# Bias in a freed row of the contraction, and expert weights loaded per block from DRAM

## The reference

```python
xn = layernorm(x)                              # 16 x 256 tokens, D = 128: each row sums to 0
s = attn(xn)                                   # mLSTM attention, 4 heads, normalised per head
logits = xn @ router_w + router_b
top1 = argmax(softmax(logits))                 # 8 experts, one for each token
h = xn @ w1[top1] + b1[top1]                   # 128 -> 1024
a, g = split(h, 2)
y = (a * sigmoid(g)) @ w2[top1] + b2[top1]     # 512 -> 128
out = x + s * silu(y)
```

## Time and profile before

| | us |
|---|---|
| median of 3 runs (281.29 to 282.22) | 281.92 |
| span of the profiled execution | 281.2 |
| PE busy | 246.7 |
| DVE busy | 191.9 |
| ACT busy | 166.7 |
| POOL busy | 125.1 |

### The profile page before, as it was taken

How to read it: one execution, slowest core, us unless ns; L and a number is a source line. 1 busy time by engine, 2 the same in 40 slices (tenths; PEclk the granted TensorE clock), 3 DMA queues, 4 the chain that set the end, 5 groups by cost and what they waited for, 6 DMA issues and landing times.

```text
span 281.2 us, 6001 instructions
## 1 busy us (share of the span) xinstructions
PE 246.7 (88%) x1640; PEld 210.6 (75%) x1640; DVE 191.9 (68%) x637; ACT 166.7 (59%) x511; POOL 125.1 (44%) x163
## 2 busy tenths in 40 slices
PE   0499969999999999999999999699999999997860
PEld 0379956776677677678889999699999899996510
DVE  3995264367764454455578798969999988967092
ACT  0143063775578778778577777377676677782030
POOL 5352000233588887884102432624463436537241
PEclk9996565697999999999999999799999999999995
DMA  7799995423144354455000110110112011000395
GB/s 201 213 368 336 288 180 83 146 77 118 53 164 136 122 147 145 122 145 153 14 1 21 50 43 28 39 56 15 52 40 60 19 53 48 21 25 16 112 313 173
DMA packets 31008, 30.92 MB, mean 110 GB/s; under 512 B 3294, under 2 KB 25830, under 8 KB 30976
## 3 DMA queue, kind: packets, MB, share of 16 engines
q1 hardware_dynamic: 27456, 26.19, 33.6%
q0 software_dynamic: 2272, 4.22, 4.3%
q10 hardware_dynamic: 1248, 0.13, 0.3%
HBM read 21.58 MB, written 9.41 MB: 110 GB/s over the span
## 4 chain that ended last, share of the span: by engine, by line
PE 59%; DVE 18%; issue 7%; DMA 4%; ACT 4%; SPq 2%; DVEq 2%; POOL 1%; ACTq 0%; POOLq 0%
PE bank L1033 15%; PE bank L1042 10%; PE bank L1001 10%; PE bank L959 8%; PE bank L900 3%; DVE dm L838 3%; DMA x_sb<-in_L_attn_x 2%; PE bank L938 2%; PE bank L942 2%; PE bank L987 2%; ACT dm L530 2%; DVE xw L595 2%; PE bank L1007 2%; DMA xw<-y_tokens 2%; PE bank L894 1%
## 5 line engine op out<-in xcount | busy, mean ns | idle before, releaser
L1033 PE MATMUL bank<-qm,wc 128*128 128x128 f32 x624 | 77.0, 276 | 0.6 <-DVE wc L711 0.6
L402 POOL DMA_INDIRECT y_tokens<-qm,xs_sb x39 | 41.7, 1070 | 75.5 <-DVE qm L855 72.9
L1033 PEld LDWEIGHTS bank<-qm,wc 128*128 128x128 f32 x624 | 73.4, 193 | 1.0 <-DVE wc L711 1.0
L1042 PE MATMUL bank<-w_sb,dm 128*128 x312 | 43.3, 283 | 5.6 <-DVE dm L838 5.2
L838 DVE SCALAR_TENSOR_TENSOR dm<-bank,wc,dm 128x128 f32<-128x128 f32 x156 | 43.7, 343 | 4.9 <-ACT dm L530 4.8
L530 ACT ACTIVATE dm<-bank,wc 128x128 f32<-128x128 f32 x156 | 43.9, 364 | 1.1 <-PE bank L1033 1.1
L1042 PEld LDWEIGHTS bank<-w_sb,dm 128*128 128x128 f32 x312 | 38.7, 195 | 7.7 <-issue 7.6
L462 ACT ACTIVATE qm<-bank 32x256 f32<-32x256 f32 x64 | 24.0, 375 | 21.4 <-PE bank L938 20.8
L397 POOL DMA_INDIRECT xs_sorted<-xw,pos x32 | 31.4, 982 | 11.5 <-issue 8.1
L478 ACT ACTIVATE dm<-mb,tm 128x128 f32<-128x128 f32 x120 | 36.5, 390 | 0.0
L959 PE MATMUL bank<-qm,xnT 128*128 128x512 f32 x64 | 32.9, 637 | 0.0
(11 more groups left out here) (168 smaller groups left out, 343.2 us busy)
## 6 DMA issues: line engine op xcount, KB each, us to landing
mb<-minus_max SPq DMA_DIRECT2D x15, 512.0 KB, 3.9
w_sb<-in_L_ffn_w SPq DMA_DIRECT2D x8, 512.0 KB, 7.5
xs_sorted<-pad_row SPq DMA_DIRECT2D x1, 2515.5 KB, 19.7
xs_sb<-xs_sorted SPq DMA_DIRECT2D x13, 193.5 KB, 2.5
x_sb<-in_L_attn_x SPq DMA_DIRECT2D x8, 256.0 KB, 4.9
xw<-y_tokens SPq DMA_DIRECT2D x8, 256.0 KB, 4.4
out_x<-xw SPq DMA_DIRECT2D x8, 256.0 KB, 3.4
y_tokens<-qm,xs_sb POOLq DMA_INDIRECT x39, 2.3
```

What stands on the lines that cost most here:

```text
L402: pool.indirect_dma_start(y_dram, bass.IndirectOffsetOnAxis(ap=xs_sb[:, j // CH % NX, j % CH, D:DW].bitcast(I32), axis=0), ys_sb[:, j // C ...
L1033: last = pe.matmul(bank[2 * (j % 2) + k][:, c * P:(c + 1) * P], wc[:, j % 3, m:m + P], xsT[:, j % 2, :], start=True, stop=True)
L1042: last = pe.matmul(bank[6 + j % 2][:, 0:D], uT[:, j % 2, c, :], w2_sb[:, bass.ds(e * (HC * D) + c * D, D)], start=(c == 0), stop=(c == HC ...
```

## The change

Each row of `xn` sums to 0, so its last element is minus the sum of the others. With row 127 of `w1[e]` subtracted from rows 0 to 126, the last element isn't needed, and row 127 of the contraction is free: `xsT` gets 1.0 there, and the folded weights get `b1[e]`. So the biases of `product` and of the sigmoid go, and each becomes one instruction over 512 columns. The folded weights of all experts are written to DRAM, and for each block SP reads the expert's number into a register and loads 512 KB from there into `wc`.

DVE makes the subtraction (`fold_row`) behind the outputs of batches 4 to 11, one expert each. SP loads row 127, broadcast to all partitions, into the three `wc` buffers in turn, and writes the eight folded matrices behind the last load of `mb`. The loads of token rows and of weights share SP's list: first four chunks of rows, then the weights of each block, and behind those of blocks 7, 10, and so on up to 31 a further chunk of rows.

```diff
@@ sync engine @@
             for e in range(E):
-                sp.dma_start(w1_sb[:, e, 0:H2], w1[e]).then_inc(s_w1, 16)
+                sp.dma_start(w1_sb[:, e, :], w1[e]).then_inc(s_w1, 16)
...
                 sp.dma_start(mb[:, b % 2, :, :], m_dram[NH * b:NH * (b + 1), :].partition_broadcast(P)).then_inc(s_mb[b % 2], 16)
-
-            sp.wait_ge(s_scat, 16 * T)
-            for c in range(NCH):
+                if b == 1:
+                    sp.wait_ge(s_w1, 16 * E)
+                    sp.dma_start(w1_sb[P - 1:P, :, :], b1.unsqueeze(0)).then_inc(s_b1, 16)
+                e = b - 1 if b <= 3 else b - 4
+                if e < 3 and b <= 3 or 3 <= e < E:
+                    if e >= 3:
+                        sp.wait_ge(s_sub, e - 2)
+                    sp.dma_start(last_row[:, e % 3, :], w1[e, D - 1:D, :].partition_broadcast(P)).then_inc(s_bc[e % 3], 16)
+
+            sp.wait_ge(s_b1, 16)
+            for e in range(E):
+                sp.wait_ge(s_sub, e + 1)
+                sp.dma_start(w1_dram[e], w1_sb[:, e, :]).then_inc(s_wd, 16)
+
+            def load_rows(c):
                 if c >= NX:
                     sp.wait_ge(s_xsp, (c - NX + 1) * CH)
                     sp.wait_ge(s_yst[c % NX], 16 * CH * (c // NX))
...
+            def load_w(j):
+                e = sp.value_load(bexp_i[0:1, j:j + 1], min_val=0, max_val=E - 1)
+                if j >= 3:
+                    sp.wait_ge(s_h, j - 2)
+                sp.dma_start(wc[:, j % 3, :].unsqueeze(1), w1_dram[bass.ds(e, 1), :, :].rearrange("e p h -> p e h")).then_inc(s_wl[j % 3], 16)
+
+            sp.wait_ge(s_scat, 16 * T)
+            for c in range(NX):
+                load_rows(c)
+            sp.wait_ge(s_bexp, 1)
+            sp.wait_ge(s_wd, 16 * E)
+            for j in range(NBLK):
+                load_w(j)
+                if j % CH == 1 and NX <= (j + 5) // CH < NCH:
+                    load_rows((j + 5) // CH)
@@ pool: one more memset @@
+            pool.memset(xsT[:, :, :], 1.0).then_inc(s_ones, 1)
@@ scalar engine: copy_w and the b1 load are gone @@
-                act.activation(xsT[:, j % 2, :], bank[4][:, 0:P], ACT.Copy).then_inc(s_xse, 1)
+                act.activation(xsT[0:P - 1, j % 2, :], bank[4][0:P - 1, 0:P], ACT.Copy).then_inc(s_xse, 1)
...
-                    for c in range(HC):
-                        last = act.activation(sg[:, j % 2, c, :], bank[2 * (j % 2) + 1][:, c * P:(c + 1) * P], ACT.Sigmoid,
-                                              bias=wc[:, j % 3, H2 + HC + c:H2 + HC + c + 1])
-                    last.then_inc(s_th, 1)
+                    act.activation(sg[:, j % 2, :, :].rearrange("p c t -> p (c t)"), bank[2 * (j % 2) + 1][:, :],
+                                   ACT.Sigmoid).then_inc(s_th, 1)
@@ vector engine: copy_w and L612 are gone @@
+                    elif b - 4 < E:
+                        fold_row(b - 4)
+
+            def fold_row(e):
+                if e == 0:
+                    dve.wait_ge(s_w1, 16 * E)
+                dve.wait_ge(s_bc[e % 3], 16 * (e // 3 + 1))
+                w = w1_sb[0:P - 1, e, :]
+                dve.tensor_tensor(w, w, last_row[0:P - 1, e % 3, :], ALU.subtract).then_inc(s_sub, 1)
...
-                for c in range(HC):
-                    last = dve.scalar_tensor_tensor(uT[:, j % 2, c, :], bank[2 * (j % 2)][:, c * P:(c + 1) * P],
-                                                    wc[:, j % 3, H2 + c:H2 + c + 1], sg[:, j % 2, c, :], ALU.add, ALU.mult)
-                last.then_inc(s_uu, 1)
+                flat = "p c t -> p (c t)"
+                dve.tensor_tensor(uT[:, j % 2, :, :].rearrange(flat), bank[2 * (j % 2)][:, :], sg[:, j % 2, :, :].rearrange(flat),
+                                  ALU.mult).then_inc(s_uu, 1)
@@ tensor engine: the b1 transpose is gone @@
-                pe.wait_ge(s_wc, j + 1)
+                pe.wait_ge(s_wl[j % 3], 16 * (j // 3 + 1))
...
-                    if k == 0:
-                        pe.wait_ge(s_wv, j + 1)
```

More of the change, by code:

```diff
@@ L59, in mlstm_moe_block @@
     y_dram = nc.dram_tensor("y_tokens", (NTOK, D), F32).ap()
+    w1_dram = nc.dram_tensor("w1_folded", (E, P, H2), F32).ap()
     m_dram = nc.dram_tensor("minus_max", (R, S), F32).ap()
@@ L79, in mlstm_moe_block @@
         u_all = sb("u_all", [P, T, NH, DA])
-        w1_sb = sb("w1_sb", [P, E, WB])
-        wc = sb("wc", [P, 3, WB])
+        w1_sb = sb("w1_sb", [P, E, H2])
+        wc = sb("wc", [P, 3, H2])
+        xsT = sb("xsT", [P, 2, D])
         w2_sb = sb("w2_sb", [P, E * HC * D])
@@ L174, in mlstm_moe_block @@
         sy = qflat[:, 8 * D:10 * D].rearrange("p (i d) -> p i d", i=2)
-        xsT = qflat[:, 10 * D:12 * D].rearrange("p (i d) -> p i d", i=2)
         sg = dm[:, 0, :, :, :]
         uT = dm[:, 1, :, :, :]
+        last_row = wc
         wflat = dm[:, 1, :, :, :].rearrange("p k h s -> p (k h s)")
@@ L200, in mlstm_moe_block @@
         s_w2 = sem("s_w2")
+        s_b1 = sem("s_b1")
+        s_bc = [sem(f"s_bc{i}") for i in range(3)]
+        s_sub = sem("s_sub")
+        s_wd = sem("s_wd")
+        s_wl = [sem(f"s_wl{i}") for i in range(3)]
         s_chain = sem("s_chain")
@@ L268, in mlstm_moe_block @@
         s_out = sem("s_out")
-        NSMALL = 11
+        NSMALL = 10
         block = ctx.enter_context(nc.Block())
@@ L495, in attention @@
                         decay(b + 1)
-            act.wait_ge(s_ones, 2)
+            act.wait_ge(s_ones, 3)
             attention()
[L499 to L509, removed]
             def evac_xs(j):
@@ L610, in _ @@
                               wbd[:, :].rearrange("p (h d) -> p h d", h=NH),
[L611 to L612 removed]
+                              vmean[:, :].unsqueeze(2).to_broadcast([P, NH, DH]), ALU.add).then_inc(s_wts, 1)
             dve.wait_ge(s_lg, 1)
@@ L670, in _ @@
             dve.wait_ge(s_tm, 1)
-            dve.wait_ge(s_ones, 2)
+            dve.wait_ge(s_ones, 3)
             def routing(part):
@@ L857, in _ @@
             dve.wait_ge(s_w2, 32)
+            dve.wait_ge(s_bexp, 1)
             normals = normalise_all(range(len(GROUPS)))
@@ L917, in _ @@
             pe.transpose(bank[4][:, P:2 * P], natbd[:, 2, :], ident[:, :])
-            pe.transpose(bank[4][:, 2 * P:2 * P + 2 * NH], gates_raw[:, 0:D], ident[0:2 * NH, 0:2 * NH])
-            pe.transpose(bank[5][:, 0:E * (WB - H2)], b1_nat[:, :], ident[0:E * (WB - H2), 0:E * (WB - H2)]).then_inc(s_wT, 1)
+            pe.transpose(bank[4][:, 2 * P:2 * P + 2 * NH], gates_raw[:, 0:D], ident[0:2 * NH, 0:2 * NH]).then_inc(s_wT, 1)
             keep_warm(2, 7)
@@ L1017, in _ @@
             pe.matmul(bank[7][:, E * T:2 * E * T], tril[:, :], ohf, start=True, stop=True).then_inc(s_cnt, 1)
-            pe.wait_ge(s_ones, 2)
+            pe.wait_ge(s_ones, 3)
             attention()
```

22 lines of the change are left out of this document (removed).

## The result

| | before | changed |
|---|---|---|
| median, us (range) | 281.56 (278.85 to 282.22) | 297.7 (295.97 to 299.02) |
| span of the profiled execution | 281.24 | 294.2 |

With the runs made beside the changed kernel, before has five. The changed kernel takes 1.0625 times as long (1.0564 to 1.0687). The forecast was 286.9 with a range up to 295: the sign is right, the size is not. The device time lies 1.75 us above the span in each execution. That puts the profiled one of before at about 283.0, above all five of its times, while that of the changed kernel is the lowest of its five; so the traces differ by 13.0 us and the medians by 16.1. What follows explains the 13.0. Ratios compare fast executions alone: one that took over 1.5% more than the fastest of its kernel is left out.

A forecast was written before the change was run, and what follows sets the result against it. Prediction: POOL bounds the attention's even batches, PE the experts' stage, with 11.0 us of stalls mostly behind DVE. -10.5 - 1.0 + 8.0 + 5.0 + 1.5 + 2.0 = +5.0 us gives 286.9 us, range 279 to 295.

The forecast's parts named there:

- folds: Attention: each of eight DVE subtractions holds POOL's L379 up by 1.0 us, and POOL has no slack; +8.0 us.
- start of the experts' stage: First L1033 waits for the eight writes, then a register read and block 0's weight load; +5.0 us (2.5 to 9).
- slow clock there: Start of the experts' stage: PE runs slow behind a gap without work; +1.5 us (0 to 3).
- gaps behind row chunks: Experts' loop: at every third block a weight load queues behind SP's y scatter wait; 4.5 x 0.4 = +2.0 us.
- DVE's relief: Experts' stage: DVE saves some 1.1 us a block, giving back 10.5 of 11.0 us of stalls; -10.5 us.
- behind the last L1042: End of the kernel: the silu and the four last scatters come earlier; -1.0 us (0 to -2).
- the third rival: Experts' loop: loads bound it, sharing DMA engines; stall 2.1 instead of 0.4, 9.5 us in all, 294.4; chance 0.15.
- L379 starts where `fold_row` ends: Attention, expected sign in the changed profile: POOL's L379 begins at the fold's end, about 1.0 us late.
- folds cost nothing: Attention, rival: POOL is already in its next batch before a fold, or isn't blocked; 278.9 us; chance 0.17.
- The clock didn't fall behind the folds: Attention, rival denied here: pauses at folds put PE's clock down at half of the eight; +5.6, 292.5; chance 0.10.
- The relief was no smaller than it looked: Experts' stage, rival denied here: DVE stays late for normalising steps, 5 of 11 us come back; 292.4; chance 0.05.

The follow-up runs named there:

- e1_rows_later: Changed kernel with SP issuing each later chunk of token rows three blocks later, same bytes; 285.47 us, ratio 1.0177 to the kernel before.
- e6_fixed_expert: Changed kernel with the expert of SP's weight load fixed as j modulo 8, no register read, wrong weights for most blocks; 294.13 us, ratio 1.0351.
- e10_quarter_loads: Changed kernel with each block's weight load cut to a quarter of the columns, 128 KB instead of 512, SP's list unchanged; 287.42 us, ratio 1.0162.
- e2_no_fold: Changed kernel with the fold's subtraction replaced by a copy of one element per partition, waits, writes and loads kept; 289.1 us, ratio 1.0279.
- e3_fold_after_evac: Changed kernel with fold_row moved ahead of the outputs, where POOL is in its scatters; 297.33 us, ratio 1.0633.
- e4_early_writes: Changed kernel with each folded matrix written one batch behind its fold and the first three weight loads ahead of the token rows; 287.67 us, ratio 1.0256.
- e5_both: Changed kernel with later row chunks three blocks later, early writes, and the first three weight loads ahead of the token rows; 279.28 us, ratio 0.9898.
- the better kernel: Changed kernel with folds moved ahead of the attention and weights copied on chip by DVE and ScalarE, no folded weights in DRAM; 273.29 us, ratio 0.9679.

## Why the prediction missed the size

The terms of the sum, on the profiled executions, which differ by 13.0 (12.9 by the rounded terms):

| term | forecast | measured |
|---|---|---|
| folds | +8.0 | +5.7 |
| attention begins earlier | 0 | -0.4 |
| start of the experts' stage | +5.0 | +6.5 |
| slow clock there | +1.5 | +2.1 |
| gaps behind row chunks | +2.0 | +9.3 |
| DVE's relief | -10.5 | -10.7 |
| behind the last L1042 | -1.0 | +0.35 |
| sum | +5.0 | +12.9 |

*Gaps, the step that failed in size.* The mechanism was written out: the load of block j+1 behind a wait for a scatter of block j-5, at every third block. Its series was too short at each link. For block 14, t0 is 183.18, the end of block 10's hidden. The scatter of block 8 was issued at 185.48, t0 + 2.3 (forecast 2.4). It landed at 188.75, t0 + 5.6 (5.0): 3.3 us, where I had taken 2.6 from a view of before in which little ran beside it (2.1 to 3.2, with a DMA share of 0.11). Rows were issued at 188.81, the load at 189.95, t0 + 6.8 (5.8): a register read of 0.7 us where I had put 0.4 for read and issue. It landed at 194.21, t0 + 11.0 (9.8), in 4.26 us instead of 3.9 and a little. PE wanted it at 189.93 + 2.79 = 192.72, t0 + 9.5 (9.4). The stall was so small a difference of two large sums (0.4) that 1.2 us more in the first made it 1.6; that it is gone at every other place held roughly (five gaps of 1.56 on the mean, four of 0.2). I had this case as the third rival, with a load at t0 + 11.5, 9.5 us and a chance of 0.15. That should have been the forecast: the scatter's landing and the load's had been priced on rows with less traffic, the register read by guess, and the change itself brings the traffic. To say "the traffic is under the rate above" answered whether the bytes fit, not how long one transfer then takes. e1_rows_later takes out the wait, e6_fixed_expert the register read and e10_quarter_loads most of the bytes; each shrinks the gaps, the first and the last to nothing or nearly so.

*Folds.* The mechanism was right (e2_no_fold), and so was reading the scatter's row at 163.56 for it (e3_fold_after_evac). The size was 0.7 a batch instead of 1.0: I had L411 start as the fold ends, but it starts 0.36 us into the fold and ends 0.26 us behind it, so what counts is its stretching from 0.42 to 1.12 us. "L379 starts where `fold_row` ends" was wrong in this detail.

*Start.* The writes ran at 354 GB/s, faster than the 325 taken, but the first landed only 5.5 us after its issue instead of about 3.6 by my figures; on the old clock the last was there at 140.6 (139.4 forecast). That first write was issued 0.43 us behind the last `mb` load, which itself took 4.6 us to land. The register read and the issue took 1.04 instead of 0.4, the landing 3.4 instead of 3.9. That the token rows queue behind the writes I had said, but not that PE would stand for them first: 3.32 us, ahead of the 2.58 for the weights. e4_early_writes shows that all this and the slow clock vanish if the writes are begun behind their folds and the first loads go ahead of the rows.

*Slow clock.* It is at 0.50 from 144.7 to 154.9; the first two periods cost 1.8 and 0.3. It fell in the 3.32 us without work ahead of the token rows, and was down already when the 2.58 us ahead of the first hidden began. The length of a pause alone doesn't tell what follows: waits of 1.42 to 1.66 us in the loop left the clock at 1.00, those of 2.03 (e4_early_writes) and 2.08 us (e6_fixed_expert) stood right ahead of a stretch at 0.50, and the 0.70 us of the earlier trace rows, from which I had worked, ended 1.8 us ahead of one.

*Relief.* 10.7 against 10.5: the stage takes 119.5 us from the first to the last group, 107.8 at the pace of 2.79, plus 9.3 of gaps, 2.1 of clock and 0.3 of DVE. That a DVE with slack would leave no stalls was right, to 0.3 us. But I had read the stalls of before as a DVE with too much to do, and named POOL's gamma product for the row at 254.20 alone. The stall at 180.26 also stands behind a DVE step, one of the normalisation, that is held up beside a gamma product, in before:

```profile
176.06 3.03 DVE L562 TENSOR_SCALAR ra<-veps 128x32 int32<-128x32 int32 x1
...
176.66 2.38 POOL L410 TENSOR_TENSOR u_all<-cm,gamma 128x1024 f32<-128x1024 f32 x1
```

Such a step takes 0.18 us elsewhere. The stalls behind the four gamma products of before (at 176.66, 206.15, 233.16 and 253.72, with DVE instructions of 3.03, 2.13, 1.73 and 2.06 us beside them) add up to 7.2 of its 11.0 us. In e5_both the same four meetings are there, and PE keeps its pace:

```profile
180.65 2.37 POOL L445 TENSOR_TENSOR u_all<-cm,gamma 128x1024 f32<-128x1024 f32 x1
...
180.85 2.22 DVE L579 TENSOR_SCALAR ry<-ra 128x32 int32<-128x32 int32 x1
...
180.99 1.95 PE L1041 MATMUL bank<-xsT,wc 128*128 128x128 f32 x16
183.78 1.95 PE L1041 MATMUL bank<-xsT,wc 128*128 128x128 f32 x16
```

So what the lighter DVE buys is mostly the slack that takes four blocks of 2 us. Whether the kernel before would gain as much with its gamma products placed elsewhere was not tried.

*End.* I had the last silu and scatters come earlier behind the last L1047. They don't: the first of the four comes behind POOL's gamma product at 266.77 and the DVE product L863 that it held up for 1.78 us, and from there they are a series of POOL's own with 0.3 between them. Before, the same series held only 0.4 us more of waiting.

*The other rivals.* That folds cost nothing fell with e2_no_fold. The clock didn't fall behind the folds: it is 1.00 over the eight batches with PE waiting about 0.6 us for L411 in each. The relief was no smaller than it looked.

*Range.* The terms' errors don't cancel: the gaps are 7.3 over, start, clock and end 3.5, the folds 2.3, the attention's earlier beginning 0.4 and the relief 0.2 under, 7.9 in all. The rest of the 10.8 us by which the median missed is where the profiled executions lie among their runs. I had set the span of before beside the median, as if it were that execution's time, and called it 0.7 under; with the 1.75 us around it, it is 1.4 over. What makes runs of one kernel differ by this much isn't known from these traces. The range ended at 295 because only one of the open terms was taken at its upper end at a time.

## What to carry to other kernels

A load in an in-order issue list inherits every wait ahead of it. Give a wait for recent work a place where nobody behind it is in a hurry, and price the series with transfers as slow as the new traffic makes them. Take a change apart before judging it: here the merged instructions gave the gain, the way over DRAM gave nothing even with its list in order, and the folds' 5 us were gone once they stood ahead of the attention (the first hidden starts 0.8 us later than before in the better kernel, less than the attention's beginning differs from trace to trace); with these three settled the same idea goes from 6% slower to 3% faster. A DVE instruction with both inputs in SBUF is priced by what POOL does at that time, not by DVE's own idle time. And a stall that is put down to a busy engine may be another engine holding it: look at the one instruction that is too long.

## What the runs showed of the hardware

- SP takes 0.7 us more to issue a load whose address comes from a register that it must first read (1.13 against 0.42 us behind the rows).
- A DVE tensor_tensor of 1.22 us with two SBUF inputs stretched an indirect scatter on POOL from 0.96 to 1.82 us, and a POOL tensor_tensor from 0.42 to 1.12; they overlapped for 0.99 and 0.86 us, so nearly the whole overlap was lost.
- A POOL tensor_tensor of 2.38 us held DVE the other way round: steps of 0.18 us beside it took 1.7 to 3.0 us in before (L562, L566, L565).
- An indirect scatter of 64 KB lands in 2.3 us (median) with few other bytes, in 3.3 to 3.7 beside a 512 KB load for each block (DMA share 0.63 in the changed kernel), and in 2.8 beside a quarter of it. The 512 KB loads took 3.1 us at least and 4.4 in the median, 3.6 in e1_rows_later. The estimate from the Trainium skill, page "DMA: Bandwidth & Descriptors", section "Anatomy of one DMA", which is for POOL's path, 3.2 us, is near the least and not the median here. With 128 KB they took 2.4.
- Eight writes of 512 KB from SBUF to DRAM landed 1.48 us apart, and the first 5.5 us after its issue, 0.43 us behind a 512 KB load that took 4.6.
